# Heads' output projection in high and low parts, with its schedule, and first scores of the second layer in other banks

## The reference, cut to what matters

```python
xn = layernorm(x)
q, k, v = heads(xn)                       # 16 heads of 64
p = softmax(causal(q @ k.T / 64))
y = p @ v
z = einsum('dvh,bhcv->bcd', W, y) * (sqrt(128 / 64) / 16) # the heads' output projection
x = x + z + shared_ffn(xn) + moe(xn)      # 32 experts, top 6, dense here; two experts to a unit
```

## Time and profile before

| | |
|---|---|
| median of 3 runs (least, most) | 1219.95 us (1219.45, 1222.29) |
| profiled execution | 1220.24 us |
| its span | 1218.4 us |
| mean granted TensorE clock | 0.997 of full |
| PE / DVE / ACT / POOL busy | 98% / 81% / 67% / 34% |

### The profile page before, as it was taken

One profiled execution on the slowest core, in us unless ns is written; L12 is line 12 of the kernel. 1 busy time (PEld: TensorE's weight loads), 2 busy tenths in 40 slices (PEclk: granted clock), 3 DMA queues, 4 the chain that ended last, 5 costly groups with the idle time before them and its releaser, 6 DMA issues.

```text
span 1218.4 us, 23951 instructions
## 1 busy us (share of the span) xinstructions
PE 1193.8 (98%) x8908; PEld 889.3 (73%) x8908; DVE 992.1 (81%) x1918; ACT 821.7 (67%) x2174; POOL 410.0 (34%) x364
## 2 busy tenths in 40 slices
PE   8999999999999999999999999999999999999998
PEld 6777777767776777777767786777677767767766
DVE  6888588968896889688968896889687977888786
ACT  6785577567756775677557755775577667777775
POOL 2216510630063007300730073007200859326910
PEclk9999999999999999999999999999999999999999
DMA  7004200310041004100410041004000400000000
GB/s 256 1 29 139 91 1 29 129 55 2 29 135 49 1 30 140 43 2 29 146 38 2 29 149 35 2 30 155 29 2 30 165 18 1 10 11 18 1 11 27
DMA packets 44292, 63.93 MB, mean 52 GB/s; under 512 B 8144, under 2 KB 18384, under 8 KB 43920
## 3 DMA queue, kind: packets, MB, share of 16 engines
q1 hardware_dynamic: 44176, 62.39, 15.7%
HBM read 59.48 MB, written 2.88 MB: 51 GB/s over the span
## 4 chain that ended last, share of the span: by engine, by line
PE 81%; DVE 9%; ACT 5%; issue 2%; POOL 1%; SPq 0%; DMA 0%; ACTq 0%; DVEq 0%; POOLq 0%
PE psum L1467 14%; PE psum L1423 14%; PE psum L1489 12%; PE psum L64 10%; PE psum L66 9%; PE psum L65 9%; PE psum L1526 4%; ACT probs L745 2%; PE psum L1432 2%; DVE mneg L1113 2%; PE psum L1375 1%; PE psum L1493 1%; DVE sg L1163 1%; DVE stats L1222 1%; DVE sg L1153 1%
## 5 line engine op out<-in xcount | busy, mean ns | idle before, releaser
L745 ACT ACTIVATE probs<-psum,mneg 128x512 f32<-128x512 f32 (+3 forms) x640 | 330.3, 530 | 134.5 <-DVE mneg L1113 130.2
L1113 DVE TENSOR_REDUCE mneg<-psum 128x2 f32<-128x1024 f32 (+2 forms) x320 | 253.6, 820 | 104.2 <-PE psum L1432 103.9
L1467 PE MATMUL psum<-ident,probs 128*128 128x128 f32 x1600 | 224.4, 278 | 8.5 <-ACT pt L766 3.1
L1104 DVE COPY pt<-psum 128x512 f32<-128x512 f32 x320 | 205.8, 682 | 30.7 <-PE psum L1467 28.4
L1467 PEld LDWEIGHTS psum<-ident,probs 128*128 128x128 f32 x1600 | 176.4, 140 | 42.1 <-issue 23.6
L552 POOL TENSOR_TENSOR qk_lo<-sg,qk_hi 128x512 fp32r<-128x512 f32 x64 | 92.4, 1450 | 162.7 <-ACT qk_hi L789 162.7
L1489 PE MATMUL psum<-pt,v_all 128*64 128x384 f32 (+5 forms) x1088 | 142.6, 412 | 0.0
L516 POOL TENSOR_TENSOR rstd<-var,mhalf 128x4 f32<-128x4 f32 x7 | 7.1, 1014 | 399.8 <-DVE var L999 399.8
L745 ACT ACTIVATION_READ_ACCUMULATOR probs<-psum,mneg 128x1 f32 x640 | 132.0, 206 | 0.0
L1423 PE MATMUL psum<-qk_hi 64*128 64x512 f32 (+7 forms) x640 | 121.4, 375 | 1.3 <-ACT probs L745 1.1
L1489 PEld LDWEIGHTS psum<-pt,v_all 128*64 128x64 f32 (+1 forms) x1088 | 69.5, 135 | 66.2 <-issue 50.7
(11 more groups left out here) (269 smaller groups left out, 2428.8 us busy)
## 6 DMA issues: line engine op xcount, KB each, us to landing
crow<-weights SPq DMA_DIRECT2D x256, 128.0 KB, 2.9
rrow<-sums SPq DMA_DIRECT2D x128, 128.0 KB, 2.9
gu_raw<-in_gu SPq DMA_DIRECT2D x1, 2176.0 KB, 11.4
x_all<-in_x SPq DMA_DIRECT2D x8, 256.0 KB, 6.4
out_rows<-x_all SPq DMA_DIRECT2D x7, 256.0 KB, 2.3
down_raw<-in_down SPq DMA_DIRECT2D x1, 1088.0 KB, 13.6
wqkv_raw<-in_wqkv SPq DMA_DIRECT2D x1, 896.0 KB, 6.7
wqkv_raw<-in_wqkv SPq DMA_DIRECT2D x1, 512.0 KB, 4.9
```

The lines of the kernel that those rows point to most:

```text
L745: last = act.activation(probs[:, h * HALF + PROB[t]:h * HALF + PROB[t] + w], bank[score_bank(rnd, c) + h][:, o:o + w], ACT.Exp, bias=mneg[ ...
L1104: dve.tensor_copy(turned_rows(rnd)[:, s % 2, :, 3 - s // 2, :], bank[TURN_BANK[s]].rearrange("p (j q) -> p j q", q=P)).then_inc(pt_ready, 1)
L1113: last = dve.tensor_reduce(mneg_h[:, :, t], psum[:, b:b + 2, o:o + P * (t + 1)], AX, ALU.max, negate=True)
L1467: last = nc.tensor.transpose(bank[TURN_BANK[s]][:, i * P:(i + 1) * P], probs[:, v:v + P], ident[:, :])
```

## The change

- `w_out0` is rounded once by ACT and split by POOL (batch 0); `project_out` uses `split_matmul`. The heads' rows get a high part `y_hi` (ACT, `high_values`, in the room of `pt`, pairs in reverse) and a low part `y_lo` (in the room of `yt`): pairs 0 to 3 on POOL behind divisions 4, 5 and 6, pairs 4 to 7 on DVE behind units 14 and 16. In the last batch all low values follow the last unit's low part, mixed with the second layer's first statistics.
- To make room, `rrow` has two rows, RROWS is 2, a third tile is listed in `probs`; `acc_cols`, `stats`, `ss1` and `rn1` move into other tiles.
- After the last unit of batch 7: down 14, 15 and 16 first, then the four projection calls, spread over the second layer's start.
- Second layer: the first round's chunks use banks 6, 0, 6; its first chunk goes ahead of `lin_out(2, 0)`; turns of batch 1's Q and K move from round 0 to round 1; ACT signals each normalized tile to PE; POOL's and DVE's lists are reordered there; one turn uses bank 6 in some rounds.

```diff
-RROWS = 3
+RROWS = 2
...
-        rrow = sb("rrow", [P, RROWS, T])
+        rrow = sb("rrow", [P, 2, T])
+        rrow0 = [rrow[:, 0, :], rrow[:, 1, :], probs[:, 4 * T:5 * T]]
...
+        def own_bank(n, s):
+            return n >= ROUNDS0 and s == 2 and (n - ROUNDS0) % (2 * G) in range(2, 2 * G, 2)
...
-            return 6 if n >= ROUNDS0 and first_round(n) and c == 1 else SCORE_BANK[c]
+            return [6, 0, 6][c] if n >= ROUNDS0 and first_round(n) else SCORE_BANK[c]
...
+        Y_HIGH_AFTER = {8: [0], 11: [1, 2], 12: [3], 13: [4], 14: [5], 15: [6], 16: [7]}
+        POOL_Y_LO = {4: [0], 5: [1, 2], 6: [3]}
+        VECTOR_Y_LO = {14: [4], 16: [5, 6, 7]}
+        LAST_POOL_Y_LO, LAST_VECTOR_Y_LO = [[0, 1], [4]], [[2, 3], [5, 6, 7]]
...
-                    sp.dma_start(rrow[h * DQ:(h + 1) * DQ, n % RROWS, :], ...
+                    sp.dma_start(rrow0[n % RROWS][h * DQ:(h + 1) * DQ, :], ...
...
+            def low_values(b, pairs):
+                for p in pairs:
+                    pool.wait_ge(y_hi_ready, b * PAIRS + p + 1)
+                    pool.tensor_tensor(y_lo[:, p, :], yt[:, p, :], y_hi[:, PAIRS - 1 - p, :].bitcast(F32), ALU.subtract).then_inc(pool_y_lo_ready, 1)
...
                         divide_pair(b, p)
+                        if b < B - 1:
+                            low_values(b, POOL_Y_LO.get(p, []))
...
+                if q == 0:
+                    low_wait(pool, B * UNITS - 1)
+                    low_values(B - 1, LAST_POOL_Y_LO[0])
                 inv_sqrt(0, 0)
...
-                inv_norms(1, 1)
                 inv_sqrt(2, 2)
                 inv_sqrt(2, 3)
+                inv_norms(1, 1)
...
+            def high_values(b, pairs):
+                for p in pairs:
+                    act.wait_ge(y_divided, b * PAIRS + p + 1)
+                    act.activation(y_hi[:, PAIRS - 1 - p, :], yt[:, p, :], ACT.Copy).then_inc(y_hi_ready, 1)
...
-                square_qk(3)
+                row_maxima(ROUNDS0 + n0 * 2, 0)
                 take_ffn(0)
                 take_ffn(1)
-                row_maxima(ROUNDS0 + n0 * 2, 0)
+                square_qk(3)
                 row_maxima(ROUNDS0 + n0 * 2, 1)
...
-                pe.wait_ge(y_divided, b * PAIRS + 2 * i + 2)
                 for p in (2 * i, 2 * i + 1):
-                    last = mm(ACC, w_out0[:, p, :], yt[:, p, :], start=False, stop=(p == PAIRS - 1), **K)
+                    last = split_matmul(nc, ACC, (w_out_hi[:, p, :], w_out_lo[:, p, :]), (y_hi[:, PAIRS - 1 - p, :], y_lo[:, p, :]), False, p == PAIRS - 1, **K)
...
-            project_out(B - 1, 0)
             unit_down(B - 1, UNITS - 3)
...
             unit_down(B - 1, UNITS - 2)
             lin_in(0, 0, 1)
-            project_out(B - 1, 1)
+            unit_down(B - 1, UNITS - 1)
+            project_out(B - 1, 0)
             lin_in(0, 0, 2)
-            unit_down(B - 1, UNITS - 1)
-            project_out(B - 1, 2)
...
                 if q == 0:
+                    project_out(B - 1, 1)
+                    turn_norm(0, 1)
+                    project_out(B - 1, 2)
+                    turn_norm(0, 2)
                     project_out(B - 1, 3).then_inc(acc_done, 1)
-                    turn_norm(0, 1)
-                    turn_norm(0, 2)
...
                 lin_in(q, 2, 2)
-                turn_norm(2, 0)
                 lin_in(q, 2, 3)
+                turn_norm(2, 0)
                 turn_norm(2, 1)
+                pe.wait_ge(qk_lo_ready, (ROUNDS0 + n0) * 2 + 2)
+                score1(0, 0)
                 lin_out(2, 0)
                 lin_out(2, 1)
                 turn_norm(2, 2)
                 turn_norm(2, 3)
-                score1(0, 0)
                 score1(0, 1)
```

More of the change, by code:

```diff
@@ L399, in build @@
         POOL_LO = {0: [], 1: [], 2: [], 3: [], 4: [], 5: [0], 6: [], 7: [1, 2], 9: [3, 4], 11: [5], 13: [6, 7]}
+        Y_HIGH_AFTER = {8: [0], 11: [1, 2], 12: [3], 13: [4], 14: [5], 15: [6], 16: [7]}
+        POOL_Y_LO = {4: [0], 5: [1, 2], 6: [3]}
+        VECTOR_Y_LO = {14: [4], 16: [5, 6, 7]}
+        POOL_YS = sum(len(v) for v in POOL_Y_LO.values())
+        LAST_POOL_Y_LO, LAST_VECTOR_Y_LO = [[0, 1], [4]], [[2, 3], [5, 6, 7]]
         def low_wait(eng, n):
@@ L840, in first_layer @@
                         act.activation(w_out0[:, :, :], w_out0[:, :, :], ACT.Copy, scale=OUT0).then_inc(act_setup, 1)
+                    if b == 0 and p == len(GU_PIECES) + 1:
+                        act.wait_ge(act_setup, 1)
+                        act.activation(w_out_hi[:, :, :], w_out0[:, :, :], ACT.Copy).then_inc(w_out_hi_ready, 1)
                 take_tile1(b * PAIRS + PAIRS - 1)
@@ L864, in first_layer @@
                             take_values(b + 1, range(2 * (u - V_AFTER), 2 * (u - V_AFTER) + 2))
+                    if b < B - 1 or u < UNITS - 2:
+                        high_values(b, Y_HIGH_AFTER.get(u, []))
                 high_part(b * UNITS + UNITS - 1, UNITS - 1)
+                if b == B - 1:
+                    high_values(b, range(PAIRS - 2, PAIRS))
             def take_ht(q, g, first=0):
@@ L900, in norm @@
                         c = (n0 + g) * TILES + t
-                        last = act.activation(zn[g][:, t, :], rows(bank[g])[:, t, :], ACT.Identity, scale=rstd[:, c:c + 1], bias=nmr[:, c:c + 1])
-                    last.then_inc(zn_ready, 1)
+                        act.activation(zn[g][:, t, :], rows(bank[g])[:, t, :], ACT.Identity, scale=rstd[:, c:c + 1], bias=nmr[:, c:c + 1]).then_inc(zn_ready, 1)
                 def gelu(k, g):
@@ L960, in _ @@
                             exps(n, c)
-                    if first and g + 1 < G:
+                    if first and 0 < g < G - 1:
                         round_q(ROUNDS0 + n0 + g + 1, 1.0)
@@ L966, in _ @@
                         exps(n, 0)
-                    if first and g + 1 < G:
+                    if r == 1:
+                        round_q(ROUNDS0 + n0 + 1, 1.0)
+                    if r == 1 or first and 0 < g < G - 1:
                         round_k(ROUNDS0 + n0 + g + 1)
@@ L1163, in hidden, with low_values @@
                 dve.tensor_tensor(sg[u % 3], sg[u % 3], crow[:, m % CROWS, :], ALU.mult).then_inc(hm_ready, 1)
+            def low_values(b, pairs):
+                for p in pairs:
+                    dve.wait_ge(y_hi_ready, b * PAIRS + p + 1)
+                    dve.tensor_tensor(y_lo[:, p, :], yt[:, p, :], y_hi[:, PAIRS - 1 - p, :].bitcast(F32), ALU.subtract).then_inc(y_lo_ready, 1)
             def add_rows(b):
@@ L1317, in _ @@
                         invert_sums(n - 1)
-                    if r == 1 or first and 0 < g < G - 1:
+                    if first and 0 < g < G - 1:
                         rest_q(ROUNDS0 + n0 + g + 1, 1.0)
@@ L1776, in turn_norm @@
                         pe.wait_ge(rrow_ready, n0)
-                    transpose_rows(bank[4 + g % 2], zn[g]).then_inc(znt_done, 1)
+                    for t in range(TILES):
+                        pe.wait_ge(zn_ready, ((q * BLOCKS + k) * G + g) * TILES + t + 1)
+                        last = nc.tensor.transpose(bank[4 + g % 2][:, t * P:(t + 1) * P], zn[g][:, t, :], ident[:, :])
+                    last.then_inc(znt_done, 1)
                 def lin_out(k, g):
```

100 lines of the change are left out of this document (70 added, 30 removed).

## The result

| | before | after |
|---|---|---|
| median (least, most) of 20 runs each | 1220.1 us (1216.4, 1222.29) | 1224.07 us (1220.82, 1226.63) |
| ratio, 95% interval | | 1.0032 [1.0024, 1.0039] |
| profiled execution, its span | 1220.24, 1218.4 us | 1224.15, 1222.0 us |

The change costs 4.0 us by the medians, 3.9 by the profiled executions. The forecast was 1221.5, within 0.3% of no change; the time came out just beyond that bound, inside the range of 1209 to 1233. To see where, the two traces are laid on each other: the start of the same PE product is read in both timelines and subtracted. The gate product that opens unit 16 of batch 7, for example, stood at 973.79 and stands at 982.89, 9.1 later.

What follows compares the result with a forecast made beforehand. PE, at work 98% of the span, was taken to bound the kernel. The terms -9.0 + 6.0 + 9.0 + 1.1 + 3.9 - 9.4 = +1.6 gave 1221.5 us by the median, no change; range 1209 to 1233.

Steps and rivals of the forecast that it cites:

- projection calls, batches 0 to 6: Projection in split parts: each of 28 calls takes 1.40 instead of 1.72 us, saving 0.32; -9.0 us.
- unit 12, batches 1 to 6: Two rows delay pair 2's load and unit 8's weights; PE waits 1.0 us ahead of unit 12; +6.0 us.
- batch ends, 1 to 6: Low values lengthen POOL's and DVE's lines, so the last unit's product comes late; 1.5 us a batch, +9.0.
- batch 0: Weights' rounding in ACT's line about half uncovered, and a tail wait of 0.6 us; +1.1 us.
- last batch and hand-over: Late unit 8, low values and calls after the last unit delay the first QKV product; +3.9 us.
- second layer: First scores go ahead of the last-block products, ending the 1.20 wait and low clock; 4.7 us a group, -9.4.
- The walk through batch 4: Step-by-step timing of loads and engine lines: PE starts unit 12 at 603.5, division 7 ends at 623.5.
- POOL is never last: Late loads and DVE's turns overlap, so the waits at batch ends vanish; 1211 us; chance 0.32.
- POOL and DVE block each other: Units 9 to 16, batches 1 to 6: every operation waits a turn, tail 2.9 instead of 1.5; 1230 us; chance 0.20.
- PE's clock falls at the heads: PE's waits at six heads bring stretches at clock 0.52, 1.7 us each; 1231.7 us; chance 0.07.
- The second layer gives little: The lower clock stays and squaring batch 3 early hurts; only -2.4 us a group, 1226 us; chance 0.06.

Runs made afterwards that it cites:

- no_low: Changed kernel without the low values: POOL's and DVE's subtractions left out, PE multiplies by the high values instead; 1216.03 us, ratio 0.9963.
- b_ring2: Kernel before with RROWS 2 and nothing else, the third row allotted but unused; 1227.65 us, ratio 1.0066.
- sums_later: Changed kernel with SP's load of pair 2's sums one iteration later, behind unit 8's weights; 1215.85 us, ratio 0.9965.
- sums_y4: `sums_later` with DVE's low value of pair 4 moved from behind unit 14 to behind the last unit; 1212.51 us, ratio 0.9932.
- b_second: Kernel before with only the second layer's part of the change; 1211.34 us, ratio 0.9930.
- order_rows: `order245` with POOL adding the second layer's rows after DVE's normalization of the fourth batch; 1209.29 us, ratio 0.9903.
- last_early: `sums_later` with the last batch treated like the others, low values and projection calls 0 and 1 made earlier; 1216.2 us, ratio 0.9963.
- order245: `sums_y4` with pair 1's sums also loaded one iteration later, behind unit 7's weights; 1209.64 us, ratio 0.9909.
- order_mix: `order245` with the edits of `last_mix`; 1210.63 us, ratio 0.9926.
- a_first: Changed kernel without the second layer's part of the change; 1231.14 us, ratio 1.0088.
- ring3: Changed kernel with RROWS 3, so the third listed tile is used, SP's order as changed; 1218.58 us, ratio 0.9993.
- last_mix: `sums_y4` with two of the last batch's low values and call 0 earlier, POOL's second-layer rows later; 1214.13 us, ratio 0.9943.

## Why the prediction was right, and where it was off

By its own steps, in us of the profiled executions (the second column is measured as the shift between the two traces over that stretch; waits are the shift plus what the calls save):

| step | predicted | measured |
|---|---|---|
| projection calls, batches 0 to 6 | -9.0 | -9.0: a call is 1.40; shown by `no_low` (1.24 to 1.30 a head) |
| unit 12, batches 1 to 6 | +6.0 | +5.6 (0.8, 0.9, 0.5, 1.4, 1.1, 0.9; `b_ring2` alone 6.0); shown by `b_ring2`, `sums_later` |
| batch ends, 1 to 6 | +9.0 | +7.5 (1.2, 1.1, 0.9, 1.3, 1.7, 1.4); shown by `no_low`, `sums_y4` |
| batch 0 | +1.1 | +2.5, of which 1.4 by chance of the clock |
| last batch and hand-over | +3.9 | +5.8 |
| second layer | -9.4 | -8.8; shown by `b_second` |
| sum | +1.6 | +3.6 |

**The mechanisms of the first three steps and of the second layer were right.** Together the first three lines sum to 4.1 against 6.0 predicted; the miss lies in the two after them, 8.3 against 5.0, so the errors partly cancel.

**Some of the agreement is luck.** The walk through batch 4 has the loads and the ends of POOL's and DVE's lines to a tenth of a microsecond. But in between unit 8's product ends at 600.25 in the time of the kernel before, not 599.7, and POOL's line starts at 602.96, not 602.4; its waits for loads and its turns with DVE are 0.6 less in sum, and so its end fits. The batch ends, 1.5 each in the prediction, are 0.9 to 1.7. In batch 0, less the clock, 1.1 came as predicted, but as a tail of 1.05 where 0.6 stood; the rounding of the weights, priced at 0.5, can't be seen (unit 0 starts 0.13 earlier than before). And the second layer's 9.4 counted in a stretch at the lower clock that not every execution has, as told below.

**The term that was mis-sized is "Last batch and the hand-over", +3.9.** Its first half held: 2.3 were given to the late loads, 2.4 measured. In the second, 1.6 were left for all that follows unit 16 and 3.4 came. The waits of PE there, in the fence above: 1.88 ahead of unit 14's down product, where call 0 used to lie, 0.57 that was there before, 0.59 for POOL's first low values, 0.16 for DVE's, and 0.62 for the normalization of the fourth batch. The prediction named the first two low values and gave the normalization no price. It took 1.11 before and takes 4.0 here (999.32 to 1003.33, of which the row below has the last three operations), since by then POOL had come to its rows, and the two took turns; here these are POOL's last operations ahead of the QKV products and DVE's:

```profile
999.41 1.37 POOL L675 TENSOR_TENSOR v_all<-v_all,x_all 128x512 f32<-128x512 f32 x1
1000.74 2.51 POOL L675 TENSOR_TENSOR room<-room,x_all 128x512 f32<-128x512 f32 x2
```

```profile
999.57 3.76 DVE L1308 TENSOR_SCALAR yt<-x_all,mv,rstd 128x128 f32<-128x128 f32 x3
```

That is 2.9 us more on DVE, but PE pays little of it: `order_rows` takes it away and gains 0.4. The larger part is that no call fills PE's first wait: `last_early` puts the calls back and is 1.0 to 2.1 shorter there, with a new wait of 2.1 included. `no_low` says that this first wait is not one for low values, since it stays (2.05). The prediction said itself that PE now stands there, and does not say how much of its 1.6 that is; so which of its numbers was short beyond the 0.4 stays open. Some of the 3.4 is chance: the wait of 1.88 is 0.95 to 1.85 in the five runs whose last batch is the same up to there and whose weights come in time, and the stretch is 2.3 longer than before in `sums_y4` and 2.6 in `order245`.

**The rivals.** "POOL is never last" fell: POOL's line ended where the walk had it. "POOL and DVE block each other", as the prediction built it, would have cost 2.9 at each batch end; the blocking is there (1.75 and 1.78 in turn), but batch ends cost 1.25 on average, for the walk had already counted most of it. "PE's clock falls at the heads" did not happen: in the window of batch 4 it is 1.00, and in no execution of these runs does a stretch below full clock lie at the head of batches 2 to 7. The waits listed there in the changed kernel are 0.2 to 0.8 each. In the hand-over, where PE's wait is longer, it did fall in some runs, as the last section has it. "The second layer gives little" fell by `b_second`.

**The trace of one execution holds a chance.** Of the second layer's 9.4, 3.4 were a stretch at the lower clock level in each group, taken as part of the kernel before. It is not in every execution. `b_ring2` leaves that stretch of the program as it was, has the same wait of 1.20, and keeps its clock; the windows are 4 us wide from 1036:

```profile
1038.41 0.66 PE L1375 MATMUL psum<-ident,yt 128*128 128x128 f32 x4 [1.20 <-ACT yt L901]
```

```profile
1036.00:1040.00 4.00, 2.80 (x26) 1.99 (x23) 2.03 (x4) 3.14 (x8) 3.84 (x7) 1.00 0.00 0
1040.00:1044.00 4.00, 4.00 (x43) 3.61 (x41) 3.20 (x4) 3.96 (x11) 3.92 (x3) 1.00 0.02 4
```

Group one is 113.93 long (first QKV product to the next group's) in the kernel before and 112.24 here, 1.69 less; group two likewise, 110.31 and 108.62 (to PE's last product). The changed kernel's groups are 3.1 and 2.4 shorter than `b_ring2`'s. So the order of the first scores is worth 3.1 and 2.4, and the clock 1.7 more where it would have fallen.

## What to carry to other kernels

A DMA queue that issues in line is a schedule: a buffer taken from its ring doesn't slow its own load, but what stands behind that load, and the cure can be one number in the list of issues. Cheap elementwise work moved to POOL and DVE to relieve PE is free only while one of the two has gaps; where both lines are full, each operation costs both engines its time, so price what comes after the moved work at its contended duration, and then ask who waits for it: here an operation group grew by 2.9 us and PE paid 0.4 of it. Before a stretch of low clock in a profile is counted as a gain, look for it in a second execution.

## What was not expected of the hardware

**The clock falls by chance after the same wait.** In batch 0 PE waits 0.68 to 0.73, ending between 116.5 and 119.5 us, in 11 of the 14 profiled executions (both kernels and the twelve others). In 8 of the 11 its granted clock then falls to 1.2 GHz for 3.4 us, and everything behind is 1.4 later: in the changed kernel, and in `b_second`, which doesn't touch that place, but not in the kernel before. In the three without that wait (`order245`, `order_mix`, `order_rows`) it never fell there. Windows of the kernel before, then of `b_second`:

```profile
116.00:120.00 4.00, 3.29 (x20) 2.85 (x21) 3.93 (x7) 2.59 (x6) 2.47 (x2) 1.00 0.54 172
120.00:124.00 4.00, 4.00 (x19) 3.24 (x18) 3.15 (x3) 2.19 (x5) 2.84 (x3) 1.00 0.64 208
```

```profile
116.00:120.00 4.00, 3.27 (x20) 2.53 (x19) 3.93 (x8) 2.39 (x6) 1.27 (x1) 1.00 0.62 188
120.00:124.00 4.00, 4.00 (x12) 3.15 (x11) 2.39 (x3) 2.11 (x6) 2.46 (x2) 0.57 0.73 199
```

The same after the 1.20 at the groups' first scores: with the old order it fell in both groups of the kernel before, in neither of `b_ring2`, in the second of `a_first`.

A third place is the hand-over. In seven executions PE waits 1.8 to 3.0 us ahead of unit 14's down product, and in five of them (`sums_later`, `ring3`, `no_low`, `a_first`, `order_mix`) the clock is at the lower level around or behind it for some 3.4 us, in `ring3` for 6.8; not in the changed kernel, nor in `last_mix`, nor where that wait is 0.95 to 1.47. `sums_later`:

```profile
978.00:981.40 3.40, 3.40 (x13) 2.65 (x12) 3.27 (x8) 2.26 (x4) 1.38 (x2) 0.50 0.02 5
```

So a hand-over read from one of these traces can be long for this alone. With the stretches that come and go a time moves by up to 1.4 to 1.7 us each, which is likely, but not shown, to be much of what single executions of one kernel differ by.

**A load can land 1.4 us late.** In `sums_y4` one load of 128 KB landed after 4.5 us, where the median is 3.1; with one load moved an iteration on, the longest took 3.8. That it was the row of loads ahead of it is likely but not shown, for the kernel before issues as long a row there.
